# The first stage of a two-layer graph network: who takes the mean off x, and where the inverse deviation goes in

## The reference, cut to what matters

```python
h = jnp.maximum(_layernorm(x, axis=-1), 0.0)        # (x - mean) / sqrt(var + 1e-5), then relu
x = x + _L0_gnn_ref(h, adj, embed, layer, embed_bias, layer_bias)
h = jnp.maximum(_layernorm(x, axis=-1), 0.0)
x = x + _L1_gnn_ref(h, adj, beta1, beta2)

def _L0_gnn_ref(x, adj, embed, layer, embed_bias, layer_bias):
    h = h_mul(x, embed)                             # exp_map_zero(log_map_zero(x) @ W)
    h = h_add(h, embed_bias[None, :])
    neigh = exp_map_zero(adj @ log_map_zero(h))
    out = h_mul(jnp.concatenate((x, neigh), axis=1), layer)
    return h_add(out, layer_bias[None, :])

def log_map_zero(y): n = _norm(y); return jnp.arctanh(jnp.clip(n, 0.0, MAX_TANH)) * y / n
def exp_map_zero(v): n = _norm(v); return jnp.tanh(n) * v / n
```

## Time and profile before

| | us |
|---|---|
| median of 3 runs (lowest to highest) | 981.88 (978.26 to 982.6) |
| the profiled execution | 978.14 |
| its span | 976.6 |
| TensorE busy in it | 929.2 (95%) |
| VectorE busy | 818.8 (84%) |
| ScalarE busy | 511.2 (52%) |
| first aggregation product starts at | 57.41 |

### The profile page before, as it was taken

How to read it: one execution, slowest core, us unless ns; L and a number is a source line. 1 busy time by engine, 2 the same in 40 slices (tenths; PEclk the granted TensorE clock), 3 DMA queues, 4 the chain that set the end, 5 groups by cost and what they waited for, 6 DMA issues and landing times.

```text
span 976.6 us, 22955 instructions
## 1 busy us (share of the span) xinstructions
PE 929.2 (95%) x9012; PEld 695.3 (71%) x9012; DVE 818.8 (84%) x2110; ACT 511.2 (52%) x756; POOL 8.0 (1%) x21
## 2 busy tenths in 40 slices
PE   2989999999996999999999999999999999999996
PEld 2944444444444878888888888778888888888885
DVE  7891888888889987888989898998778887888887
ACT  1711122212126685766656667787565565656564
POOL 0000000000000000000000000000000000000000
PEclk9899999999998999999999999999999999999999
DMA  8338988888861445565465555545565655665630
GB/s 301 143 118 285 307 285 287 277 295 283 301 229 44 174 173 207 196 246 212 179 235 192 222 217 193 180 167 217 197 217 198 246 197 204 221 232 189 246 142 36
DMA packets 29971, 207.26 MB, mean 212 GB/s; under 512 B 3632, under 2 KB 4272, under 8 KB 5296
## 3 DMA queue, kind: packets, MB, share of 16 engines
q1 hardware_dynamic: 28224, 203.44, 57.6%
q0 software_dynamic: 640, 2.10, 0.5%
q10 hardware_dynamic: 1008, 0.33, 0.1%
HBM read 203.75 MB, written 2.10 MB: 211 GB/s over the span
## 4 chain that ended last, share of the span: by engine, by line
PE 69%; DVE 22%; issue 5%; ACT 3%; DMA 1%; DVEq 0%; POOL 0%; SPq 0%; POOLq 0%
PE s_ps L622 17%; PE s_ps L608 10%; PE acc_ps L469 6%; PE acc_ps L675 6%; PE acc_ps L671 6%; PE acc_ps L673 6%; PE acc_ps L652 5%; PE acc_ps L648 5%; PE acc_ps L650 5%; DVE small L1132 1%; DVE small L1134 1%; DVE small L1133 1%; DVE work L1647 1%; ACT work L990 1%; PE s_ps L427 1%
## 5 line engine op out<-in xcount | busy, mean ns | idle before, releaser
L990 ACT ACTIVATE work<-s_ps,beta_bias,beta_scale 128x1024 f32<-128x1024 f32 x144 | 173.4, 1204 | 217.0 <-PE s_ps L622 216.9
L469 PE MATMUL acc_ps<-ring,set 128*128 128x512 f32 x512 | 223.8, 596 | 3.2 <-DVE set L1245 3.2
L1665 DVE SCALAR_TENSOR_TENSOR h_all<-ring,s_ps 128x1024 f32<-128x1024 f32 x112 | 136.7, 1221 | 65.5 <-PE s_ps L608 64.3
L469 PEld LDWEIGHTS acc_ps<-ring,set 128*128 128x128 f32 x512 | 96.8, 191 | 120.3 <-issue 117.6
L1647 DVE TENSOR_TENSOR work<-work 128x1024 f16<-128x1024 f32 x96 | 132.5, 1380 | 5.4 <-ACT work L1000 5.4
L1000 ACT ACTIVATE work<-work 128x1024 f16<-128x1024 f32 x96 | 131.5, 1369 | 3.2 <-DVE work L1655 0.2
L1655 DVE SCALAR_TENSOR_TENSOR work<-ring,work 128x1024 f32<-128x1024 f32 x96 | 116.8, 1217 | 0.0
L622 PE MATMUL s_ps<-xt 128*128 128x512 f16 x432 | 106.4, 382 | 3.8 <-ACT work L990 3.0
L622 PE MATMUL s_ps<-set 128*128 128x512 f16 x432 | 105.0, 379 | 0.5 <-ACT work L990 0.5
L671 PE MATMUL acc_ps<-set,work 128*128 128x129 f16 x576 | 102.4, 219 | 2.7 <-DVE accs L1682 2.7
L671 PE MATMUL acc_ps<-src,work 128*128 128x129 f16 x576 | 103.5, 220 | 1.4 <-DVE work L1655 1.4
(11 more groups left out here) (260 smaller groups left out, 1723.2 us busy)
## 6 DMA issues: line engine op xcount, KB each, us to landing
ring<-in_adj_t SPq DMA_DIRECT2D x192, 1024.0 KB, 5.0
x_sb<-in_x SPq DMA_DIRECT2D x4, 512.0 KB, 7.2
out<-x_sb POOLq DMA_DIRECT2D x8, 256.0 KB, 2.8
w<-in_layer ACTq DMA_DIRECT2D x2, 64.0 KB, 8.1
w<-in_embed ACTq DMA_DIRECT2D x1, 64.0 KB, 4.2
eb<-in_embed_bias ACTq DMA_DIRECT2D x1, 64.0 KB, 6.9
lb<-in_layer_bias ACTq DMA_DIRECT2D x1, 64.0 KB, 7.9
beta<-in_beta ACTq DMA_DIRECT2D x2, 0.5 KB, 7.2
```

The costliest lines, as they stand in the source:

```text
L469: last = nc.tensor.matmul(agg, v_sb[:, jb, :], ring[:, k, b, :], start=jb == 0, stop=jb == NB - 1)
L990: nc.scalar.activation(values[x.n % VR], score_ps, ACT.Exp, bias=beta_bias[:, x.la:x.la + 1], scale=beta_scale[:, x.la:x.la + 1]).then_inc ...
L1665: V.scalar_tensor_tensor(turned[x.off % MR].rearrange("p (b j) -> p b j", b=CB), ring[:, x.mir_tile % AR, :, ds(x.h * HB * P, HB * P)], 0. ...
```

## The change

ScalarE takes over (x - mean) with the relu for six of the eight groups, part by part as x's statistics are made: max(x - mean, 0) with the negated mean as bias. VectorE does the two late groups (XS_LATE = 6). The inverse deviation no longer enters here; being positive it passes through relu, transposition and products, and is multiplied in later: into hh as its square, into the factor of the embed product (sm(2)), and into h1 as a scale when ScalarE copies it out, four copies for each group instead of one. It is kept in ext, and is worked out behind the late groups. The product with the bias is no longer a product of its own: web is the 129th column of w1, so that the g product has 129 columns (PW), and the copy to scr_a takes it along. VectorE forms web between the first and the second part of x. TensorE waits for web and no longer for embed at its start. It runs idle products of 128 by 128: ten (WAKE) ahead of the first transposes, two (FILL) behind each group's g product, 18 (WARM) ahead of the aggregation. The transposed groups have three buffers instead of two, and the order of ScalarE's program is written out anew, with the first logarithms ahead of the last two g_out and the second ones behind five h1_out instead of four.

```diff
     QP = 32
-    WARM = 10
+    WARM = 18
+    FILL = 2
+    XS_LATE = 6
+    WAKE = 10
...
         adj_rows = work[:, 0:N]
-        scr_a = work[:, 0:NB * F].rearrange("p (b f) -> p b f", f=F)
+        scr_a = work[:, 0:NB * PW].rearrange("p (b w) -> p b w", w=PW)
+        gb_sb = scr_a[:, :, F]
         scr_b = xt0[:, :, :].rearrange("p s n -> p (s n)").bitcast(f32)[:, 0:NB * F].rearrange("p (b f) -> p b f", f=F)
...
-        w1 = sb("w1", [F, 2 * F])
+        w1 = sb("w1", [F, 2 * F + 1])
+        web = w1[:, F:F + 1]
         w2 = sb("w2", [F, F])
...
         ht_sb = src0_all[:, 0:2 * N].bitcast(f32)
-        web = sb("web", [F, 1])
         ones_h = sb("ones_h", [P, P], f16)
...
-        g_ps = [s_ps[:, i, 0:CH].rearrange("p (b f) -> p b f", f=F) for i in range(2)]
+        g_ps = [s_ps[:, i, :].rearrange("p (k n) -> p k n", k=2)[:, :, 0:2 * PW] for i in range(2)]
         h1_ps = [s_ps[:, i // 2, ts(i % 2, CH)].rearrange("p (b f) -> p b f", f=F) for i in range(4)]
-        gb_ps = acc_ps[:, 0, 0:NB]
+        idle_ps = acc_ps[:, 1, 0:P]
         w_ps = s_ps[:, 0, 0:CH].rearrange("p (b f) -> p b f", f=F)
         xt_ps = s_ps[:, 1, 0:CH]
-        ht_ps = [acc_ps[:, 2 + i, :] for i in range(2)]
+        ht_ps = [acc_ps[:, i, :] for i in (0, 2, 3)]
         rows_ps = s_ps[:, 0, CH:2 * CH].rearrange("p (b f) -> p b f", f=F)
...
         g_done = sem("g_done")
-        gb_done = sem("gb_done")
+        means_made = sem("means_made")
+        xs_late = sem("xs_late")
+        deviations_made = sem("deviations_made")
         h1_done = sem("h1_done")
...
             pe.wait_ge(consts_made, 6)
-            pe.wait_ge(embed_in, 16 * 2)
-
+
+            def idle_products(n):
+                for _ in range(n):
+                    nc.tensor.matmul(idle_ps, ident[:, :], ident[:, :], start=True, stop=True)
...
             def h_transposes(r):
-                pe.wait_ge(xs_ready, r + 1)
-                wait(pe, ht_copied, r - 1)
-                for b in range(CB):
-                    last = nc.tensor.transpose(ht_ps[r % 2][:, ts(b, P)], scr_b[:, r * CB + b, :], ident[:, :])
+                if r < XS_LATE:
+                    pe.wait_ge(xs_ready, r + 1)
+                else:
+                    pe.wait_ge(xs_late, r + 1 - XS_LATE)
+                wait(pe, ht_copied, r - 2)
+                for b in range(CB):
+                    last = nc.tensor.transpose(ht_ps[r % 3][:, ts(b, P)], scr_b[:, r * CB + b, :], ident[:, :])
                 last.then_inc(ht_done, 1)
...
+            idle_products(WAKE)
             h_transposes(0)
...
                     h_transposes(r + 1)
+                if r == 0:
+                    pe.wait_ge(web_made, 1)
                 pe.wait_ge(ht_copied, r + 1)
...
                 for b in range(CB):
-                    last = nc.tensor.matmul(g_ps[r % 2][:, b, :], ht_sb[:, ts(r * CB + b, P)], w1[:, 0:F],
-                                            start=True, stop=True)
+                    last = nc.tensor.matmul(g_ps[r % 2][:, b // 2, ts(b % 2, PW)], ht_sb[:, ts(r * CB + b, P)],
+                                            w1[:, 0:PW], start=True, stop=True)
                 last.then_inc(g_done, 1)
-                if r == 0:
-                    pe.wait_ge(web_made, 1)
-                for b in blocks(r):
-                    last = nc.tensor.matmul(gb_ps[:, b:b + 1], ht_sb[:, ts(b, P)], web[:, :], start=True, stop=True)
-                last.then_inc(gb_done, 1)
+                idle_products(FILL)
...
                 for b in range(CB):
-                    last = nc.tensor.matmul(h1_ps[r % 4][:, b, :], ht_sb[:, ts(r * CB + b, P)], w1[:, F:2 * F],
+                    last = nc.tensor.matmul(h1_ps[r % 4][:, b, :], ht_sb[:, ts(r * CB + b, P)], w1[:, ds(PW, F)],
                                             start=True, stop=True)
...
-            for _ in range(WARM):
-                nc.tensor.matmul(acc_ps[:, 1, 0:P], ident[:, :], ht_sb[:, 0:P], start=True, stop=True)
+            idle_products(WARM)
             aggregate(0, 0, False, False)
...
                 .then_inc(embed_in, 16)
-            for dst, s in ((w1[:, F:2 * F], layer[0:F, :]), (w2[:, :], layer[F:2 * F, :]),
+            for dst, s in ((w1[:, ds(PW, F)], layer[0:F, :]), (w2[:, :], layer[F:2 * F, :]),
                            (lb[:, :], layer_bias.rearrange("(a f) -> a f", a=1).to_broadcast([P, F])),
...
                     q = r * CB + b
-                    nc.scalar.activation(h1_sb[:, q, :], g_ps[r % 2][:, b, :], ACT.Square,
+                    nc.scalar.activation(h1_sb[:, q, :], g_ps[r % 2][:, b // 2, ds(b % 2 * PW, F)], ACT.Square,
                                          accum_out=small[:, 10, q:q + 1])
-                nc.scalar.activation(scr_a[:, ts(r, CB), :], g_ps[r % 2], ACT.Copy).then_inc(g_copied, 1)
+                nc.scalar.activation(scr_a[:, ts(r, CB), :].rearrange("p (k b) w -> p k (b w)", k=2), g_ps[r % 2],
+                                     ACT.Copy).then_inc(g_copied, 1)
...
                     act.wait_ge(g_copied, NC)
-                nc.scalar.activation(h1_sb[:, ts(r, CB), :], h1_ps[r % 4], ACT.Copy).then_inc(h1_copied, 1)
+                    act.wait_ge(deviations_made, 1)
+                for b in range(CB):
+                    q = r * CB + b
+                    last = nc.scalar.activation(h1_sb[:, q, :], h1_ps[r % 4][:, b, :], ACT.Copy, scale=ext[:, q:q + 1])
+                last.then_inc(h1_copied, 1)
...
             nc.scalar.activation(unused[:, 0, 0:1], ones[:, 0:1], ACT.Ln)
-            for r in range(NC):
+            def x_rows(i):
+                act.wait_ge(means_made, i + 1)
+                for r in range(i * NC // XP, (i + 1) * NC // XP):
+                    for b in blocks(r):
+                        last = nc.scalar.activation(scr_b[:, b, :], x_sb[:, b, :], ACT.Relu, bias=small[:, 7, b:b + 1])
+                    last.then_inc(xs_ready, 1)
+
+            def h_out(r):
                 act.wait_ge(ht_done, r + 1)
-                nc.scalar.activation(ht_sb[:, ds(r * CH, CH)], ht_ps[r % 2], ACT.Relu).then_inc(ht_copied, 1)
-                if r:
-                    g_out(r - 1)
-            log_terms(sm(4, NB), sm(5, NB), sm(6, NB))
+                nc.scalar.activation(ht_sb[:, ds(r * CH, CH)], ht_ps[r % 3], ACT.Copy).then_inc(ht_copied, 1)
+
+            x_rows(0)
+            h_out(0)
+            x_rows(1)
+            h_out(1)
+            x_rows(2)
+            g_out(0)
+            for r in range(2, NC):
+                h_out(r)
+                if r == NC - 1:
+                    log_terms(sm(4, NB), sm(5, NB), sm(6, NB))
+                g_out(r - 1)
             g_out(NC - 1)
             on(ACT.Tanh, sm(5, NB), sm(4, NB))
-            for r in range(NC // 2):
+            for r in range(5):
                 h1_out(r)
             log_terms(sm(4, NB), sm(5, NB), sm(6, NB))
-            for r in range(NC // 2, NC):
+            for r in range(5, NC):
                 h1_out(r)
...
             for i in range(XP):
+                these = range(i * NB // XP, (i + 1) * NB // XP)
                 dve.wait_ge(x_in[i], 16)
-                for b in range(i * NB // XP, (i + 1) * NB // XP):
+                for b in these:
                     ins = V.bn_stats(stats[:, b, :], x_sb[:, b, :])
...
                 V.memset(sm(0, NB), 0.0)
-                for b in range(i * NB // XP, (i + 1) * NB // XP):
+                for b in these:
                     ins = V.bn_aggr(mean_var[:, b, :], stats[:, b, :])
-            dve.wait_ge(embed_in, 16 * 2)
-            V.scalar_tensor_tensor(bsq[:, :], w1[:, 0:F], 1.0, eb[:, :], ALU.mult, ALU.mult,
-                                   accum_out=web[:, :]).then_inc(web_made, 1)
-            step(ins)
-            step(V.tensor_scalar(sm(0, NB), mean_var[:, :, 1], LN_EPS, None, ALU.add))
-            inv_sqrt(sm(1, NB), sm(0, NB), sm(2, NB))
-            for r in range(NC):
+                step(ins)
+                if i + 1 < XP:
+                    q = slice(these[0], these[-1] + 1)
+                    V.tensor_scalar(small[:, 7, q], mean_var[:, q, 0], -1.0, None, ALU.mult).then_inc(means_made, 1)
+                if i == 0:
+                    dve.wait_ge(embed_in, 16 * 2)
+                    V.scalar_tensor_tensor(bsq[:, :], w1[:, 0:F], 1.0, eb[:, :], ALU.mult, ALU.mult,
+                                           accum_out=web).then_inc(web_made, 1)
+            for r in range(XS_LATE, NC):
                 for b in blocks(r):
-                    ins = V.tensor_scalar(scr_b[:, b, :], x_sb[:, b, :], mean_var[:, b, 0:1], small[:, 1, b:b + 1],
-                                          ALU.subtract, ALU.mult)
-                ins.then_inc(xs_ready, 1)
-            dve.wait_ge(xs_ready, NC)
-
+                    ins = V.tensor_scalar(scr_b[:, b, :], x_sb[:, b, :], mean_var[:, b, 0:1], 0.0,
+                                          ALU.subtract, ALU.max)
+                ins.then_inc(xs_late, 1)
```

(19 more changed lines are left out.)

## The result

| | before | after |
|---|---|---|
| median of 6 runs each | 978.27 | 971.67 |
| lowest to highest | 977.52 to 982.6 | 970.03 to 971.88 |
| the profiled execution (its span) | 978.14 (976.6) | 971.64 (970.1) |
| first aggregation product at | 57.41 | 50.76 |
| the 72 records from there | 32.83 | 31.14 |

The ratio of after to before is 0.991, with a 95% interval of 0.9891 to 0.9928: the change makes the kernel faster, by 0.7 to 1.1%. The medians alone are 6.60 us apart, a ratio of 0.9933 just outside this interval, for two of the six runs before lie about 4 us above the others, no run after does, and a median of six doesn't count them. The last three rows split the difference of the two profiled spans, 6.5 us: 6.65 us come from the first stage and 1.69 from the clock in the first chunk, close to the forecast (6.1 and 1.9), and 1.8 us are given back in the rest, which it did not say.

A forecast was written before the change was run, and what follows sets the result against it. The chain of waits up to the first aggregation product was taken to bound, with TensorE full from then on. 6.1 us from the first stage plus 1.9 from the clock made 8.0, set against 981.88: 973.9 us, range 969 to 979.5.

The forecast's parts named there:

- first stage: Everything up to the first aggregation product on TensorE, forecast to start at 51.3 instead of 57.41 us: 6.1 us gained.
- ScalarE's start: ScalarE's first relu, forecast at 7.5 us, once x's first quarter has its statistics and negated means.
- second block: VectorE's second block of eight statistics of x, forecast to start at 8.6 us, behind the wait for the embed bias.
- the request: VectorE's asking ScalarE for the first logarithms, forecast at 31.75 us instead of 36.66.
- the norm: VectorE's norm behind the logarithms and last two g_out, forecast to start at 35.5 us instead of 41.57.
- Rival 2: Relus, pointer copies or hand-overs on ScalarE cost more than their slack: 3.5 us of gain left, 978.4 us; chance 0.12.
- both covers: ScalarE's forecast slack: 3.2 us before the first logarithms, 1.5 us around the h1_out copies and second logarithms.
- The h1 products and the idle time: TensorE before the aggregation: h1 products take 10.2 us to 45.7, warming products to 50.0, leaving 1.3 us idle.
- The clock term: TensorE's clock stays up at the aggregation's start because less idle time precedes it: 1.9 us saved on 72 records.
- rival 1: First stage 6.1 us shorter, but TensorE's clock still falls at the aggregation: 975.8 us; chance 0.26.
- Rival 3: TensorE's clock stays low through the first loop: 992 us, or 983 if it rises in the h1 products; chance 0.05.
- Rival 4: The shift is absorbed later, at the pair stage near 300 us or another clock fall: 981 us, no change; chance 0.07.

The follow-up runs named there:

- e1: Changed kernel with VectorE doing mean and relu of all eight groups, ScalarE none (XS_LATE 0): 976.06 us, one run.
- e2: Changed kernel with 10 warming products ahead of the aggregation instead of 18: 974.05 us, one run.
- e3: Old kernel with 18 warming products instead of 10, nothing else: 979.46 us over ten runs, ratio 1.0002 to the kernel before.
- e4: Changed kernel with VectorE's embed bias product behind the second part's statistics instead of the first's: 969.91 us, one run.
- e8: Changed kernel with the bias product behind the second part's statistics and ScalarE's relus for seven groups instead of six: 970.81 us, four runs.
- e7: Changed kernel with 14 idle products where TensorE waits at the handing over to the pair stage, near 287 us: 971.9 us, five runs.
- e10: Changed kernel with eight idle products at the fifth step of the pair stage, where TensorE waits near 308 us: 970.67 us, four runs.
- e5: Changed kernel without the two idle products behind each group's g product (FILL 0): 971.76 us, one run.
- e6: Changed kernel without the ten idle products ahead of the first transposes (WAKE 0): 970.5 us, one run.
- e9: Changed kernel with 28 warming products ahead of the aggregation instead of 18: 970.55 us, four runs.
- e11: Changed kernel with later bias product, ScalarE relus for seven groups, 28 warming products, eight idle products at the pair stage's fifth step: 969.34 us, six runs.

## Why the prediction was right and wrong

**The base: the step that failed.** The sum was made against the profiled execution, 978.14 - 8.0 = 970.1, and then set on the median of the three runs shown, 981.88, to give 973.9. That median was 3.6 us above the median of all six runs, 978.27, and against this 973.9 is a gain of only 4.4 us. Measured were 6.5 us between the two profiles, 6.6 between the medians, and 8.8 by the ratio of 0.991. The working's own gain of 8.0, set on 978.27, gives 970.3. Over the whole study the kernel before has 38 runs: 26 between 977.0 and 979.1 and 12 between 981.2 and 982.7, and two of the first three were of the upper group. With a spread of 4.3 us among three runs and a profile of the lower group, the base should have been the profile's own 978.14, with the upper group as the high end of the range.

That 973.9 missed the measured 971.67 by only 2.2 us is luck: the base was 3.6 too high, and the 8.0 was 1.5 more than the 6.5 between the profiles, and the two errors went opposite ways. What the upper group is was not found out, since no run of it was profiled. Among the 34 runs of the changed kernel and of its variants there is no such group (the two above 973, e1 and e2, are accounted for by their profiles), while four of the ten of e3, which has the old first stage, are above 981.2. So the change seems to do away with the group, which the sum did not foresee, and the 8.8 us of the ratio would contain this; no profile shows it.

**The first stage** was forecast at 6.1 us and gave 6.65. Term by term: ScalarE's start 7.5 (7.71, x having landed 0.14 later), second block 8.6 (8.61), then 11.05 (11.04), start of the late groups 15.8 (15.82), the late groups 2.1 (1.58: one pointer less does cost less, the lower end that was named), the request 31.75 (31.16), ScalarE idle in front of it 3.2 (2.16), the norm 35.5 (34.87). Of the 0.6 us between forecast and measured, 0.5 are the late groups. e1 shows that VectorE's chain bounds, e4 and e8 that shortening it pays almost one to one, and e8 that ScalarE had the room. Rival 2 did not come: the relus cost the 0.31 us that was taken, the pointer copies 0.26, and both covers held (2.16 us in front of the logarithms, about 1 us between the table load and the second request).

**The h1 products and the idle time** were the second weak step. I took 10.2 us from the old run, with 6.2 of low clock; it was 9.0 (34.91 to 43.92), since the products began at the high clock and it was low for 3.4 us only, and the idle time before the aggregation was 2.66 instead of 1.3. The clock term still came out at 1.69 of 1.9 in the profile, which was luck: with 2.65 to 2.67 us of idle time it stayed up in two profiles (after, e1) and fell in three (e7, e8, e10). Of these five, the changed kernel, e7 and e10 are alike up to there, and it fell in two of the three. So rival 1 is a course that the changed kernel itself can take, in a share of its runs that nobody measured. From 3.24 us on it fell three times of three, at 2.55 and less it stayed up five times of five.

**FILL and WAKE** were costed at nothing either way (slack until about 25 us), and e5 and e6 confirm it. Rival 3 did not come: the clock was low twice in the loop (until 12.3 and from 19.2 to 22.6 us), and TensorE still had the last product ready 3 us early.

**Rival 4**, that the shift is absorbed later, had a share: 1.8 of 8.3 us, by the clock at 309 us, which I named as a place without a price. The profiles fall into two kinds, 886.4 to 886.9 us without that stretch and 887.9 to 888.4 with it, and e9 between them (887.4, with a second stretch earlier, from 301 to 308 us). The prediction set against this rival that TensorE is full for 230 us and that no engine has a time of its own. The first half is so (229.50 us busy from 57.5 to 287). But the forecast booked the rest as unchanged, and past 287 us TensorE waits for VectorE again and again and its clock falls at places that differ from kernel to kernel.

What makes the clock fall near 309 us in one kernel and not in another that differs only 250 us earlier is not settled. The idle time at 287 us does not decide it: e4, e6 and e8 have it as the changed kernel does (3.8 to 3.9 us) and no second stretch. The traces show something nearer. TensorE's idle time just before this step (1.89 in brackets at 308.54 above) was 1.89 or 1.90 us in all five profiles with the stretch, and 1.29 to 1.58 in four of the five without it and without e10's fill (before, e6, e7, e8). e4 is the exception, 1.89 without the stretch. So this idle time seems to be needed and not enough, and e10 and e11, which fill it, fit that without proving it.

## What to carry to other kernels

When a stage's engines work side by side, find the one whose chain runs through to the next stage; here moving 24 instructions of 0.21 us from it to an engine that idled bought 4.6 us, although each takes 0.31 us there. Set a sum on the time of the execution that it was read from, and look at how the shown runs lie before taking their median as the base. In this kernel idle products paid only where they closed the last gap before a long run of products (with eight of them fewer e2 lost 2.5 us there, while leaving out the others cost nothing in e5 and e6); give them enough to close it whatever the clock of the work before, and look at the clock at every later place where TensorE waits before booking the gain.

## What was not expected of the hardware

The same idle time of 2.66 us left the clock up in one profile (after) and down in another (e7) of kernels that are alike up to there. The price of a fall was 1.7 us in the aggregation (31.14 to 32.84 for 72 records) and up to 2.5 (e2), and 1.5 us where six score products ran in 2.77 instead of 1.46 us. Where VectorE set the pace, a low clock lasting 13.7 us (e6, e8) cost nothing that can be seen: 886.9 and 886.7 us for the rest, against 886.9 in e10 with 3.4 us of it.
